# A mixer and expert kernel on one core: all u score blocks moved behind the key projection, and the u masks behind the fourth lerp

## The reference, cut to what matters

```python
xrg, xwa, xk, xv = x[None] + xx[None] * (time_maa + deltas)
r = xrg @ receptance.T
g = jnp.tanh(xrg @ gate_w1.T) @ gate_w2.T
k = xk @ key_w.T
v = xv @ value.T
...
def step(S, inp):
    r_, w_, k_, v_, kk_, b_ = inp
    sab = jnp.einsum('bhvk,bhk->bhv', S, kk_)
    S = S * jnp.exp(w_)[:, :, None, :] + sab[..., None] * b_[:, :, None, :] + v_[..., None] * k_[:, :, None, :]
    y = jnp.einsum('bhvk,bhk->bhv', S, r_)
    return (S, y)
...
bonus = (r4 * k4 * time_faaaa.reshape(H, N)).sum(-1, keepdims=True) * v4
out = (yn + bonus).reshape(B, T, C) * g
return out @ output.T
```

## Time and profile before

| | |
|---|---|
| Median of three runs | 5919.83 us (5905.62 to 5934.96) |
| Span of the profiled execution | 5915.8 us |
| Around the span, median less span | 4.0 us |
| TensorE matmul, busy | 5448.2 us, 92% |
| TensorE weight load, busy | 3816.4 us, 65% |
| VectorE, busy | 3741.6 us, 63% |
| ScalarE, busy | 2017.7 us, 34% |
| GpSimd, busy | 1392.5 us, 24% |
| Mean granted TensorE clock | 0.97 of full |

### The profile page before, as it was taken

The page is one execution under the profiler, slowest core; times in us unless marked ns, Lnnn a source line. Parts: engine busy times, 40 slices in busy tenths (PEclk is TensorE's granted clock), DMA queues, the critical chain, the costliest instruction groups (busy, mean ns, idle before and its releaser), DMA issues. The chain is left out here.

```text
span 5915.8 us, 243936 instructions
## 1 busy us (share of the span) xinstructions
PE 5448.2 (92%) x110664; PEld 3816.4 (65%) x110664; DVE 3741.6 (63%) x9004; ACT 2017.7 (34%) x3659; POOL 1392.5 (24%) x1156
## 2 busy tenths in 40 slices
PE   6999999999989999998999989975999999999998
PEld 6777777777777777777777777752444444444443
DVE  6888888788878888887888877855232242232310
ACT  4444444444444444444444444430000000000000
POOL 1222222222222222222222222222022022121220
PEclk8999999999999999999999999986999999999999
DMA  1001000010000001010000001003112112112110
GB/s 62 23 18 25 18 24 19 18 25 18 25 18 20 24 18 25 18 25 18 20 24 20 23 18 25 16 14 99 50 54 99 50 52 102 47 55 96 41 64 14
DMA packets 108637, 211.07 MB, mean 36 GB/s; under 512 B 25552, under 2 KB 26704, under 8 KB 107088
## 3 DMA queue, kind: packets, MB, share of 16 engines
q1 hardware_dynamic: 92240, 144.91, 8.4%
q0 software_dynamic: 15360, 50.48, 2.6%
HBM read 144.60 MB, written 50.72 MB: 33 GB/s over the span
## 5 line engine op out<-in xcount | busy, mean ns | idle before, releaser
L392 DVE COPY_PREDICATED time_raw<-time_known,w_bank 128x96 f32<-128x96 int32 (+6 forms) x3072 | 816.7, 274 | 213.4 <-PE w_bank L1046 126.9
L1865 PE MATMUL moe_bank<-moe_w,moe_hidden 128*128 128x512 f32 x2048 | 930.4, 597 | 0.0
L1852 PE MATMUL moe_bank<-moe_hT,moe_w 128*128 128x512 f32 x2048 | 924.3, 594 | 1.5 <-DVE moe_hT L1746 1.5
L1767 ACT ACTIVATE moe_hidden<-moe_bank,moe_b 128x512 f32<-128x512 f32 x256 | 175.9, 687 | 1635.3 <-PE moe_bank L1852 1499.3
L1852 PEld LDWEIGHTS moe_bank<-moe_hT,moe_w 128*128 128x128 f32 x2048 | 386.5, 190 | 471.7 <-issue 469.8
L1865 PEld LDWEIGHTS moe_bank<-moe_w,moe_hidden 128*128 128x128 f32 x2048 | 379.8, 190 | 429.7 <-issue 428.2
L909 POOL TENSOR_TENSOR time_grow<-time_eye,time_grow 128x512 f32<-128x512 f32 x256 | 349.8, 1366 | 1160.0 <-DVE time_grow L418 1160.0
L1031 PE MATMUL w_bank<-time_ew,time_grow 32*32 32x64 f32 x32768 | 404.8, 219 | 157.3 <-issue 141.5
L1031 PEld LDWEIGHTS w_bank<-time_ew,time_grow 32*32 32x32 f32 x32768 | 351.5, 104 | 195.5 <-issue 154.1
L1046 PE MATMUL w_bank<-time_keys,time_queries_u 32*32 32x160 f32 x8192 | 366.8, 312 | 33.9 <-issue 22.4
L1746 DVE COPY moe_hT<-moe_bank 128x512 f32<-128x512 f32 x64 | 44.2, 691 | 500.9 <-PE moe_bank L1837 500.9
(11 more groups left out here) (226 smaller groups left out, 9456.5 us busy)
## 6 DMA issues: line engine op xcount, KB each, us to landing
moe_w<-in_w SPq DMA_DIRECT2D x64, 1024.0 KB, 7.4
mid_xn<-time_xn_rows SPq DMA_DIRECT2D x128, 129.0 KB, 2.7
time_x_rows<-in_x SPq DMA_DIRECT2D x128, 128.0 KB, 2.7
time_base<-in_x SPq DMA_DIRECT2D x128, 128.0 KB, 3.0
mid_acc<-time_mixed SPq DMA_DIRECT2D x128, 128.0 KB, 2.3
mid_scores<-time_rated SPq DMA_DIRECT2D x128, 2.0 KB, 1.7
moe_b<-in_b SPq DMA_DIRECT2D x8, 256.0 KB
time_key_w<-in_w_key_w SPq DMA_DIRECT2D x1, 1024.0 KB, 5.5
```

Source lines behind the costliest of these rows:

```text
L392: e.copy_predicated(by_raw[:, "uy".index(q), n0:n1, :, 0:8 * j + 8], known[:, "uy".index(q), :, :, mine].to_broadcast([P, n1 - n0, 2, 8 * ...
L1767: e.activation(hidden[now % 4][:, :], up[now % 3][:, :], ACT.Gelu_apprx_tanh, bias=b1[:, x * FC + k:x * FC + k + 1]).then_inc(act.sem, act ...
L1852: got = e.matmul(up[now % 3][:, :], w1[:, g * F + k * P:g * F + (k + 1) * P], hT[x % 2][:, g * CAP + half * HALF:g * CAP + (half + 1) * HA ...
L1865: got = e.matmul(down[t][:, :], hidden[now % 4][:, t * P:(t + 1) * P], tile(w2, k), start=k == 0, stop=k == FC - 1)
```

## The change

The same instructions are issued in another order, by TensorE and by VectorE.

- On TensorE the bonus matmuls go from before inverse stage 4 to behind it. u0 and u1, which stood between low_wa and stage 8, and u2, which stood between stage 16 and the second half of the key projection, go behind that half, so u0, u1, u2, u3 follow each other.
- On TensorE `from_state(0)` goes behind y2 and y3, and `u_of(0)` behind the first half of the output projection, directly before `from_solved(0)`.
- On VectorE the bonus product goes behind the transpose C.t4; the masks of u0, u1 and u2 go behind the fourth lerp and the three transposes of `turn_keys`; the mask of y2 goes before the transpose C.z0.
- Banks, buffers, waits within each operation, and the orders of ScalarE, GpSimd and SyncE stay.

```diff
@@ on_vector
             if A:
                 lerp_of(1)
+            if Cs:
+                turn_rest(4)
             if Bs:
                 bonus_of()
-            if Cs:
-                turn_rest(4)
             if D:
                 gated_of()
             if A:
                 lerp_of(2)
             if Cs:
                 turn_scores([(1, "uk")])
-            if Bs:
+            if Cs:
+                turn_rest(8)
+                turn_scores([(2, "yb"), (3, "yk")])
+            if A:
+                lerp_of(3)
+            if Bs:
+                turn_keys()
                 mask_scores("u", 0)
-            if Cs:
-                turn_rest(8)
-            if Bs:
                 mask_scores("u", 1)
-            if Cs:
-                turn_scores([(2, "yb"), (3, "yk")])
-            if A:
-                lerp_of(3)
-            if Bs:
                 mask_scores("u", 2)
-                turn_keys()
                 mask_scores("u", 3)
@@ on_tensor
-            if Bs:
-                bonus_of()
             if Cs:
                 inverse_stage(4, 0)
                 inverse_stage(4, 1)
+            if Bs:
+                bonus_of()
             if A:
                 low("low_wa", 1)
-            if Bs:
-                score("u", 0)
-                score("u", 1)
             if Cs:
                 inverse_stage(8, 0)
                 inverse_stage(8, 1)
@@ on_tensor
-            if Bs:
+            if A:
+                key_of(2, 4).then_inc(pe.sem, pe.step("A.key"))
+            if Bs:
+                score("u", 0)
+                score("u", 1)
                 score("u", 2)
-            if A:
-                key_of(2, 4).then_inc(pe.sem, pe.step("A.key"))
-            if Bs:
                 score("u", 3)
@@ on_tensor
-            if Cs:
-                from_state(0)
             if Bs:
                 score("y", 2)
                 score("y", 3)
             if Cs:
-                u_of(0)
+                from_state(0)
             if D:
                 clear_out()
                 out_of(0, 2)
             if Cs:
+                u_of(0)
                 from_solved(0)
```

More of the change, by code:

```diff
@@ L274, in time_mix @@
         PE_STEPS = (
-            "A.x C.S1 A.scored D.centre A.mix B.value D.var A.delta C.S2 D.gate A.gate1 B.bonus C.S4 A.low_wa B.u0 B.u1 "
-            "C.S8 A.low_k C.S16 B.u2 A.key B.u3 A.decay B.u4 B.u5 A.low2 B.y0 B.y1 A.sums C.z0 B.y2 B.y3 C.u0 C.y0 D.out "
+            "A.x C.S1 A.scored D.centre A.mix B.value D.var A.delta C.S2 D.gate A.gate1 C.S4 B.bonus A.low_wa "
+            "C.S8 A.low_k C.S16 A.key B.u0 B.u1 B.u2 B.u3 A.decay B.u4 B.u5 A.low2 B.y0 B.y1 A.sums B.y2 B.y3 C.z0 C.u0 C.y0 D.out "
             "B.y5 B.y4 C.z1 C.u1 A.recept C.y1").split()
@@ L589, in on_vector @@
                 turn_scores([(1, "uk")])
-            if Bs:
-                mask_scores("u", 0)
             if Cs:
                 turn_rest(8)
-            if Bs:
-                mask_scores("u", 1)
-            if Cs:
                 turn_scores([(2, "yb"), (3, "yk")])
@@ L600, in on_vector @@
             if Bs:
+                turn_keys()
+                mask_scores("u", 0)
+                mask_scores("u", 1)
                 mask_scores("u", 2)
-                turn_keys()
                 mask_scores("u", 3)
@@ L614, in on_vector @@
                 mask_scores("y", 1)
+            if Bs:
+                mask_scores("y", 2)
             if Cs:
@@ L617, in on_vector @@
             if Bs:
-                mask_scores("y", 2)
                 mask_scores("y", 3)
@@ L1255, in on_tensor @@
                 inverse_stage(16, 1)
-            if Bs:
-                score("u", 2)
             if A:
@@ L1260, in on_tensor @@
             if Bs:
+                score("u", 0)
+                score("u", 1)
+                score("u", 2)
                 score("u", 3)
```

## The result

| | before | after |
|---|---|---|
| Median of four runs | 5912.73 us (5902.96 to 5934.96) | 6075.84 us (6065.67 to 6079.79) |
| Ratio after to before | | 1.0256, 95% interval 1.0236 to 1.0276 |
| Span of the profiled execution | 5915.8 us | 6071.9 us |

The change makes the kernel slower by 2.6%: 152 us by the ratio, 163 by the two medians. Executions of one and the same kernel lie up to 30 or 40 us apart, and the slower of them have the lower mean clock, so a difference of 10 us, or of 0.2 us a step in one profile, says little. The direction and the range held. The forecast of 6028 was 48 us short, and this part and the next are about those 48 us.

The account below looks back on a forecast made before the run. The prediction took TensorE's order of work, through the waits it makes, as the bound: +2.9 us of waits a step less 1.1 of issue time, net +1.8, times 60 is +108 on 5919.8, giving 6028 us; range 5965 to 6110.

Parts of the forecast that it names:

- What bounds the kernel: In the mixer: TensorE's list of work has almost nothing between; order matters only through waits; 4.86 us idle a step.
- The waits: New TensorE waits a step: stage 4 0.60, stage 8 0.30, low_k 1.15, u2 0.50, u3 0.22, from_solved 0.50; together 3.27.
- What was to go: Old TensorE waits expected to vanish in each step: 0.16 us before the bonus and about 0.20 before low_k.
- the walk: Tracing one mixer step place by place in the new order: +2.9 us a step, without issue time.
- What issue time gives back: On TensorE: part of the new waits replaces waiting for instruction packets, taken as 1.1 us a step, leaving net +1.8.
- the two groups of the earlier trace: TensorE's two largest issue rows before, 138.9 + 22.4 us, or 2.9 a step, mostly in inverse stages; expected to fall to about 1.8.
- The pair of the earlier trace: Two neighbouring steps, one with a 2.0 us wait for VectorE, both 61.0 to 61.1 long; read as waits replacing issue time.
- The clock: TensorE's half-clock loss, 1.7 us a step, was left unchanged; its price was bounded between -1.7 and +3.2.
- more half clock: Rival: nothing returned, and idle time beside stage 8 lowers the clock, 1.7 us more a step; 6196 us, chance 0.05.
- The sum: Per step: 2.9 us of waits less 1.1 of issue time, clock unchanged, net +1.8; over 60 steps +108 us.
- nothing given back: Rival: issue time belongs to the dense stages alone, or is no fetching, so +2.9 us a step stays; 6094 us, chance 0.19.
- What was to be seen: Signs in the profile after: shortest step 59 to 60 us, the named waits, issue time about 1.8 a step, clock 0.96 to 0.98.

Follow-up runs that it names:

- late_xf2: The kernel before with two useless VectorE operations ahead of the third lerp, so xf2 comes late, TensorE's order untouched; 6021.77 us, ratio 1.0163.
- solve_alone: The kernel before with only the solve's moves (from_state(0), u_of(0), and VectorE's mask of y2); 5944.48 us, ratio 1.0030.
- u0_between: The changed kernel with u0 alone put between stage 8 and low_k on TensorE; 6044.04 us, ratio 1.0191.
- u_back: The changed kernel with u0, u1, u2 and their masks back in their old places, bonus and solve still moved; 5999.31 us, ratio 1.0121.
- bonus_ahead: The changed kernel with the bonus back ahead of stage 4 on TensorE and of C.t4 on VectorE; 6069.82 us, ratio 1.0242.
- split_stages: The kernel before with the halves of stages 1, 2, 8 and 16 apart on TensorE, other work between them, u2 ahead of stage 16; 5880.98 us, ratio 0.9921.
- u2_ahead: The kernel before with only u2 moved ahead of stage 16, no stage split; 5867.05 us, ratio 0.9913.

## Why the prediction was right, and where it was short

- **What bounds the kernel** was read rightly: TensorE's order of work, through the waits that it makes.
- **The waits**, place by place, as the mean of 56 steps: stage 4 0.48 (0.60 was forecast), stage 8 0.18 (0.30), low_k 0.81 (1.15), u2 and u3 0.66 (0.72), from_solved 0.47 (0.50), together 2.60 for 3.27. What was to go, 0.16 before the bonus and 0.20 before low_k, was hardly there: 0.03 a step before the bonus, and no wait of low_k for xf2 in any of the 56 steps. In its place went the 0.13 before stage 16 and small waits elsewhere. All engine waits together rose by 2.23, where the walk had 2.9.
- **"What issue time gives back", 1.1 a step, is the step that failed.** By the sign that the prediction gave itself: the two groups of the earlier trace rows were to fall from 2.9 to 1.8 and are at 3.0. All issue rows together fell by 0.12. The walk has 2.9 and idle time rose by 2.17, so about 0.7 did overlap, in a way that the prediction did not have. The stalls inside stage 8 are about as long as before (35 us in the 56 steps, 38 before), but a stall shortens the wait that comes after it. In the kernel after, 33 of the 56 steps have no issue stall inside stage 8, and low_k waits 1.37 us in them on average, more than the walk's 1.15; the other 23 have one, of 1.52 on average, and low_k waits 0.06. VectorE makes xf2 while TensorE stalls. late_xf2 has the same: 1.15 in 29 steps, 0.05 in 27.
- **The experiments bear most of this out.** Against 3.44 before, issue time is 3.40 in solve_alone and in u0_between, 3.56 in late_xf2, 3.32 in the change, 3.19 in u_back and 3.01 in bonus_ahead. In late_xf2, where a wait was added and TensorE's order left alone, it did not fall. In bonus_ahead it fell by 0.43 while the waits rose by 2.09, a fifth of them; whether the waits or the other order did that was not taken apart. The somewhat over a third that was forecast is in no run.
- **The evidence for it was misread.** The pair of the earlier trace rows was to show a step with a wait of 2.0 for VectorE and little issue time. The step 28 steps earlier has nearly the same rows. TensorE's waits from 1562.3 to 1623.3 in the kernel before:

```profile
PE w_bank L1007 <- DVE time_mixed L463: 2.0, 1, 2.0
PE w_bank L1031 <- issue: 1.3, 2, 0.9
PE w_bank L1083 <- issue: 0.4, 1, 0.4
```

  and its timeline at that place, followed by that of the step of the earlier trace rows:

```profile
1582.18 0.65 DVE L463 TENSOR_TENSOR time_mixed<-time_mixed,time_bonus 128x512 f32<-128x512 f32 x1
...
1583.52 1.13 PE L1007 MATMUL w_bank<-time_xf,time_low_wa 128*128 128x128 f32 x8 [2.01 <-DVE time_mixed L463]
```

```profile
3283.64 0.69 DVE L411 TENSOR_TENSOR time_xf<-time_lerp,time_x 128x512 f32<-128x512 f32 x1
...
3287.20 1.13 PE L1007 MATMUL w_bank<-time_xf,time_low_wa 128*128 128x128 f32 x8 [2.00 <-DVE time_mixed L463]
```

  low_wa reads xf1, complete at 3283.64 + 0.69 = 3284.33, and nothing of `mixed`. TensorE stood still until 3287.20 for something that no engine did. It is issue time under another name, in the same instruction of a loop body of 28 steps, both times it ran. So the first step of the pair holds 2.0 of issue time besides its 1.3, and the pair showed two steps with the same kind of stall, and no exchange. (Waits under a wrong name come to some 0.26 a step before and 0.14 after; with them, issue time fell by about 0.25.)
- **The clock**, left as it is, was the other error: +0.37 a step. The times agree: of the 152 us, 60 x 2.17 = 130 are idle time. Two neighbouring steps of the kernel after show its price by themselves:

```profile
2074.70:2135.50 60.80, 54.67 (x1650) 44.75 (x1650) 50.43 (x126) 28.66 (x53) 16.11 (x13) 1.00 0.08 21
2135.50:2199.00 63.50, 58.06 (x1651) 47.91 (x1651) 50.51 (x126) 28.66 (x53) 16.13 (x13) 0.95 0.08 20
```

  The second has less idle time (5.44 against 6.13) and is 2.7 longer, at 0.95 of the clock. The rival "more half clock" put 1.7 on this and had the direction.
- **The sum**: 2.23 of waits, less 0.12 of issue, with 0.06 of small gaps and 0.37 of busy time is 2.54, against 2.9 - 1.1 + 0 = 1.8. The 0.74 between them, 60 times, is 44 of the 48 us. Both errors have the same sign and did not cancel; the time is in the range because the range took in most of "nothing given back". By its time the nearest case was the rival "nothing given back" (6094), and by its mechanism too as far as issue time goes: the overlap of 0.7 and the clock of 0.37 lie either side of it.
- **What issue time is**, the packets show. In the 56 steps before, 734 packets of instructions of 16 KiB arrive. TensorE has 130 issue stalls of over 0.5 us in them, and 98% of these end 1.2 to 1.6 us after such a packet has landed; of moments taken at random, 9% lie so. In the change all of its 109 do, but of the 35 waits over 0.5 us that the profile puts down to an xf only one does. So the issue time is a wait for instructions, as the prediction read it. The Trainium skill, "Runtime: NRT & Kernel Launch", section "Instruction fetch mechanics", has the fetches mostly hidden, because the sequencer issues more slowly than blocks arrive. The trace agrees for most packets and not for all: 130 stalls for 734 packets, and 3.44 us of issue time a step; and split_stages, which issues the same instructions in another order, has 1.15 less of it.
- **What was to be seen**: the shortest step has 60.4 instead of 59 to 60, the clock is within 0.96 to 0.98, the waits are before stages 4 and 8 (in 45 and 34 of 56 steps, where "nearly every step" was said), low_k, u2 and from_solved as named; the stages' and u blocks' issue time is (167.0 + 0.9)/56 = 3.0 a step instead of 1.8, the sign that was given for a wrong prediction, and with it the time leaned to the 6094 of that case.

What stays open: no run changed the number of instructions or packets, so what one packet fewer would save is not shown; and no run changed the clock by itself, so that the half clock comes of where the idle time stands is read from kernels that differ in both.

## What to carry to other kernels

Walk the order of work place by place for waits, and price a wait at its length; don't count on it to take the place of unexplained idle time, though a stall just ahead of it does shorten it, and look whether it costs busy time through the clock as well: here it did between dense stretches. Before a wait row serves as evidence, check that the instruction reads what the row names, and in a loop whether the same instruction stalls again one body later: if so, it belongs to the code and not to the engine named. And look for the sparse work that stands behind a dense stretch which has to wait: moved ahead of it, it covers that wait at no cost.

## What was not expected

- **The move that covers a wait of 0.13 was worth 55 us.** Moving u2 ahead of stage 16 took 0.13 of recorded wait and 0.20 of issue from a step, and as much again (0.38) from busy time. In the 56 steps of the kernel before TensorE's clock is granted at half for 167 us, in those of u2_ahead for 126 us, in those of the change for 201 us and of bonus_ahead for 256 us. Busy time follows it at a third to a half: from before to bonus_ahead 89 us more at half clock and 29 us more busy; from before to u2_ahead 41 us less and 21 us less.
- **Where the idle time stands matters.** solve_alone adds 0.47 of wait between two halves of the output projection and costs 18 us, with 143 us at half clock, no more than before; late_xf2 adds 0.98 of wait, before low_k and stage 16, and costs 97 us, five times as much for twice the wait. A part of that is that small waits went elsewhere in solve_alone: idle time rose by 0.30 there and by 1.14 in late_xf2, and that makes 18 and 68 us.
- **Splitting has a price of its own.** split_stages has less than half as long at half clock as before (78 us against 167), which by the above should save 0.5 to 0.8 of busy time a step, yet TensorE is busy 56.19 a step against 56.04. Why four split stages cost that much busy time, some 0.7 to 1 us, stays open; it was not tried by itself.
